# Spreading the projection work of a pair of token blocks over two attention units

## What is computed

```python
x: (32, 256, 128)                 # 32 batches, 256 tokens, width 128; 16 heads of 8
def _mha(q, k, v, ...):
    qp = (q @ wq.T + bq) * dh ** (-0.5);  kp = k @ wk.T + bk;  vp = v @ wv.T + bv
    s = einsum('bqhd,bkhd->bhqk', qh, kh)
    return einsum('bhqk,bkhd->bqhd', softmax(s), vh).reshape(B, Lq, D) @ w_out.T + b_out
# local: attention over axis 0 windows of 40 on the layer-normed x (with B = 32 only rows
# 0 to 31 of axis 1 and all 32 of axis 0); global: attention inside each of the 32 batches
x = layernorm(x + local + global)
x = layernorm(x + moe(x))         # top-1 routing over 8 experts, 1024 tokens each, 128-512-128
```

## Time and profile before

| | |
|---|---|
| median of 3 runs | 719.67 us (717.74 to 720.22) |
| the profiled execution's own time | 713.15 us |
| its span, first to last instruction | 711.4 us |
| TensorE busy (matmuls) | 633.0 us, 89% |
| VectorE busy | 561.1 us, 79% |
| ScalarE busy | 485.8 us, 68% |
| GpSimd busy | 445.1 us, 63% |
| mean granted TensorE clock | 0.949 |

### The profile page before, as it was taken

One profiled execution on the slowest core, in us unless ns is written; L12 is line 12 of the kernel. 1 busy time (PEld: TensorE's weight loads), 2 busy tenths in 40 slices (PEclk: granted clock), 3 DMA queues, 4 the chain that ended last, 5 costly groups with the idle time before them and its releaser, 6 DMA issues.

```text
span 711.4 us, 18732 instructions
## 1 busy us (share of the span) xinstructions
PE 633.0 (89%) x6430; PEld 353.5 (50%) x6430; DVE 561.1 (79%) x1722; ACT 485.8 (68%) x1095; POOL 445.1 (63%) x813
## 2 busy tenths in 40 slices
PE   3478999999999999999999999999999369999993
PEld 2344554445454454444544444444444237677682
DVE  7566899999999999999899998998972206776776
ACT  2226678888888988888878888888888234354431
POOL 5414434578788787787877877675667702544546
PEclk9657999999999999999999999999999569999997
DMA  5696889975648747666466565673401022333321
GB/s 114 157 214 173 215 232 194 249 178 124 168 134 184 176 99 208 165 140 164 111 158 179 120 160 144 131 176 73 86 26 35 27 65 73 108 97 105 96 86 40
DMA packets 143960, 95.70 MB, mean 135 GB/s; under 512 B 11885, under 2 KB 139718, under 8 KB 143865
## 3 DMA queue, kind: packets, MB, share of 16 engines
q1 hardware_dynamic: 138728, 85.82, 50.2%
q0 software_dynamic: 4096, 7.81, 3.8%
q10 hardware_dynamic: 1040, 0.87, 0.5%
HBM read 47.70 MB, written 45.74 MB: 131 GB/s over the span
## 4 chain that ended last, share of the span: by engine, by line
PE 58%; DVE 27%; issue 6%; DMA 4%; SPq 2%; POOL 2%; ACT 2%; DVEq 0%; POOLq 0%; ACTq 0%
DVE mx L1040 15%; PE ps_o L613 11%; PE ps_b L586 9%; PE ps_a L1487 7%; PE ps_b L1481 4%; PE ps_a L568 4%; PE ps_m L644 3%; PE ps_f L522 3%; PE ps_m L659 2%; PE ps_f L517 2%; PE ps_f L527 2%; PE ps_a L1481 2%; PE ps_f L1481 2%; PE ps_m L638 2%; DVE rest L1012 2%
## 5 line engine op out<-in xcount | busy, mean ns | idle before, releaser
L1040 DVE TENSOR_REDUCE mx<-ps_a 128x2 f32<-128x512 f32 (+1 forms) x576 | 360.3, 654 | 44.9 <-PE ps_a L568 43.1
L839 ACT ACTIVATE prob<-ps_b 128x512 f32<-128x512 f32 (+1 forms) x576 | 301.2, 580 | 66.4 <-PE ps_b L586 65.3
L568 PE MATMUL ps_a<-ks,qs 56*128 56x256 bf16 (+1 forms) x1152 | 186.0, 272 | 12.0 <-DMA ks<-stack 6.2
L586 PE MATMUL ps_b<-qs,ks 59*128 59x256 bf16 (+1 forms) x1152 | 187.7, 269 | 6.5 <-DMA qs<-mT 1.7
L613 PE MATMUL ps_o<-prob,vp 128*32 128x256 f32 (+1 forms) x2304 | 170.2, 379 | 0.4 <-ACT prob L839 0.4
L586 PEld LDWEIGHTS ps_b<-qs,ks 59*128 59x128 bf16 x1152 | 80.5, 95 | 105.2 <-ACT prob L839 64.5
L1631 POOL DMA_INDIRECT out<-res,dest x64 | 62.3, 973 | 76.5 <-DVE res L1604 61.1
L1334 POOL DMA_INDIRECT routed<-row,slot x64 | 67.2, 1050 | 47.7 <-issue 27.4
L568 PEld LDWEIGHTS ps_a<-ks,qs 56*128 56x128 bf16 x1152 | 75.2, 95 | 25.2 <-DVE mx L1040 13.1
L613 PEld LDWEIGHTS ps_o<-prob,vp 128*32 128x32 f32 x2304 | 49.1, 108 | 57.1 <-issue 48.6
L1487 PE MATMUL ps_a<-w_sb,prob 128*128 128x128 f32 x512 | 59.7, 275 | 2.1 <-ACT prob L1539 2.1
(11 more groups left out here) (153 smaller groups left out, 999.2 us busy)
## 6 DMA issues: line engine op xcount, KB each, us to landing
stack<-part SPq DMA_DIRECT2D x36, 384.0 KB, 3.3
qs<-stack SPq DMA_DIRECT2D x72, 192.0 KB
ks<-stack SPq DMA_DIRECT2D x72, 192.0 KB
stack<-part SPq DMA_DIRECT2D x36, 256.0 KB, 3.6
stack<-part SPq DMA_DIRECT2D x36, 128.0 KB, 4.3
routed<-empty SPq DMA_DIRECT2D x8, 520.0 KB, 4.6
rows_sb<-routed SPq DMA_DIRECT2D x16, 260.0 KB, 3.9
xt<-x SPq DMA_DIRECT2D x16, 256.0 KB, 3.1
```

Source lines behind the costliest of these rows:

```text
L568: ins = nc.tensor.matmul(ps_a[:, n % 3, qt * S:qt * S + keys.stop - keys.start], qs[half, b, hp, qt * P:(qt + 1) * P], ks[half, b, hp, key ...
L586: ins = nc.tensor.matmul(ps_b[:, 1 - e, kt * n:(kt + 1) * n], ks[half, u % STACKS, hp, kt * P:(kt + 1) * P], qs[half, u % STACKS, hp, quer ...
L839: nc.scalar.activation(prob[:, hp, half * n:(half + 1) * n], ps_b[:, half, 0:n], ACT.Exp).then_inc(exp_done, 1)
L1040: nc.vector.reduce_max(mx[:, u % 2, :, col], ps_a[:, n % 3].rearrange("p (t k) -> p t k", t=2)[:, :, 0:k], axis=AX).then_inc(max_done, 1)
```

## The change

It moves instructions within the two units of a pair; the products and their sizes are the same, except that ScalarE's `second_part` of a pair (one instruction of 128 x 1024) becomes two of 128 x 512.

On TensorE `turn_x` goes from step 1 of the even unit to the end of step 7 of the odd unit before it (for the first such pair ahead of the loop). q goes from steps 3 and 4 to 2 and 3, k from step 7 alone to 6 and 7, v from step 2 alone to 2 and 3 of the odd unit. On ScalarE `scale_shift` goes from behind exponential 2 to behind exponential 0; `second_part_q` stands in the even unit behind exponential 6, `second_part_k` in the odd one behind exponential 2; the two halves of v are placed one exponential later each; `norm_again` of an odd unit goes one exponential later. On VectorE `take_rest_k` stands ahead of maximum (1, 1) in place of maximum (2, 0).

```diff
--- before.py
+++ after.py
@@ -683,13 +683,11 @@
                     pe.wait_ge(y_ready, min(u - 1, U))
                     pe.wait_ge(logits_read, batch(u - 3) + 1)
                     count_tokens(u - 3)
-                if first is not None:
-                    turn_x(first, 0)
-                    turn_x(first, 1)
             if hp == 2:
                 if second is not None:
                     project_in(second, "v", 0)
-                    project_in(second, "v", 1)
+                if first is not None:
+                    project_in(first, "q", 0)
                 if there(u - 1):
                     if routes(u - 3):
                         pe.wait_ge(counts_copied, batch(u - 3) + 1)
@@ -706,8 +704,10 @@
                     else:
                         pe.wait_ge(mT_ready, u + 1)
                     turn_max(u + 1)
+                if second is not None:
+                    project_in(second, "v", 1)
                 if first is not None:
-                    project_in(first, "q", 0)
+                    project_in(first, "q", 1)
             if hp == 4:
                 if there(u):
                     p_v(u, 0, 1)
@@ -719,8 +719,6 @@
                     turn_oN(u - 1)
                 if routes(u - 2):
                     turn_x1(u - 2)
-                if first is not None:
-                    project_in(first, "q", 1)
             if hp == 5:
                 if there(u):
                     p_v(u, 1, 0)
@@ -728,15 +726,20 @@
                     logits(u - 2)
                 if there(u - 1):
                     project(u - 1)
-            if hp == 6 and there(u):
-                p_v(u, 1, 1)
-                p_v(u, 2, 0)
+            if hp == 6:
+                if there(u):
+                    p_v(u, 1, 1)
+                    p_v(u, 2, 0)
+                if first is not None:
+                    project_in(first, "k", 0)
             if hp == 7:
                 if there(u):
                     p_v(u, 2, 1)
                 if first is not None:
-                    project_in(first, "k", 0)
                     project_in(first, "k", 1)
+                if first_pair(u + 1) is not None:
+                    turn_x(first_pair(u + 1), 0)
+                    turn_x(first_pair(u + 1), 1)
 
         pe.wait_ge(first_loaded, 16 * len(needed_first))
         turn_first(0)
@@ -772,6 +775,8 @@
                 turn_max(0)
         project_in(OPEN, "v", 0)
         project_in(OPEN, "v", 1)
+        turn_x(AHEAD, 0)
+        turn_x(AHEAD, 1)
         for u in range(U + 3):
             for hp in range(8):
                 score_half(u, hp, 0)
@@ -813,6 +818,14 @@
             nc.scalar.copy(part[:, first:first + 12].rearrange("p (h s t) n -> p s h t n", h=2, s=2)[:, :, halves, 1],
                            rest[:].rearrange("p s (h n) -> p s h n", h=2)[:, :, halves]).then_inc(part1_ready, 1)
 
+        def second_part_q(p):
+            act.wait_ge(rest_q, upto(p))
+            nc.scalar.copy(part_of(p, 1), by_unit(rest[:, 0]))
+
+        def second_part_k(p):
+            act.wait_ge(rest_k, upto(p))
+            nc.scalar.copy(part_of(p, 4), by_unit(rest[:, 1])).then_inc(part1_ready, 1)
+
         def place_v(p, h):
 
             act.wait_ge(projected_v, p + 1)
@@ -893,6 +906,8 @@
             first, second = first_pair(u), second_pair(u)
             if there(u):
                 exponential(u, 0)
+            if first is not None:
+                scale_shift(first)
             if second is not None:
                 first_part_k(second)
             if there(u):
@@ -903,16 +918,12 @@
                 copy_o(u - 1)
             if there(u):
                 exponential(u, 2)
-            if first is not None:
-                scale_shift(first)
             if second is not None:
-                second_part(second)
+                second_part_k(second)
             if there(u):
                 exponential(u, 3)
             if there(u + 1):
                 copy_max(u + 1)
-            if second is not None:
-                place_v(second, 0)
             if routes(u - 2) and batch(u - 2) >= 3:
                 number_rows(batch(u - 2))
             if u == LU:
@@ -926,13 +937,20 @@
             if first is not None:
                 first_part_q(first)
             if second is not None:
-                place_v(second, 1)
+                place_v(second, 0)
             if there(u):
                 exponential(u, 5)
-            if routes(u - 2):
+            if second is not None:
+                place_v(second, 1)
+            elif routes(u - 2):
                 norm_again(u - 2)
             if there(u):
                 exponential(u, 6)
+            if first is not None:
+                second_part_q(first)
+            if second is not None and routes(u - 2):
+                norm_again(u - 2)
+            if there(u):
                 exponential(u, 7)
             if routes(u - 2):
                 gate_exp(u - 2)
@@ -1134,11 +1152,12 @@
                 expert_mask(u - 3)
             if at == (1, 0) and routes(u - 3):
                 gate_sum(u - 3)
-            if at == (1, 1) and routes(u - 3):
-                gate(u - 3)
-            if at == (2, 0):
+            if at == (1, 1):
                 if second is not None:
                     take_rest_k(second)
+                if routes(u - 3):
+                    gate(u - 3)
+            if at == (2, 0):
                 if late is not None:
                     input_stats(late, (2, 3) if late > AHEAD + 1 else (0, 1, 2, 3))
             if at == (3, 0):
```

## The result

The changed kernel takes 716.31 us in the median (713.73 to 719.65, 19 runs) against 719.39 us (716.38 to 724.15, 18 runs) of the kernel before on the same chip: ratio 0.9957, 95% interval 0.9938 to 0.9975. A nineteenth run of the kernel before took 962.15 us, a slow one, and is left out. That is 3.1 us less, where 6.8 were forecast: the sign and the range were right, the size was less than half.

A forecast was written before the change was run, and what follows sets the result against it. Bound: the hand-over between TensorE and the two readers of its scores. Waits fall 0.50 us a pair: 6.0 over twelve pairs, 0.40 last odd unit, 0.4 first three, sum 6.8, so 712.9 us; 8 in 10 from 706.5 to 720.5.

The forecast's parts named there:

- TensorE's waits: Waits of TensorE in a pair's two units: 1.36 us before, 0.86 after, so 0.50 less a pair.
- step 0: Even unit, second maxima product: its 0.25 us wait goes, since `turn_x` moves ahead and VectorE catches up.
- Step 1's second half: Even unit, second half of the scores, waiting for exponential 0: 0.22 of its 0.33 us wait stays.
- Step 2's: Even unit, second half of the scores: new 0.36 us wait, as `scale_shift` delays exponential 1.
- Step 3: Even unit, second half of the scores: its 0.22 us wait goes, with q put in the step before.
- It adds no product on TensorE, so its load stays.: TensorE over a pair: with no product added, its load was taken as unchanged, and only waits were priced.
- ScalarE's split copies: `second_part` as two copies of 512 columns: 0.04 to 0.26 us more for ScalarE a pair, nothing on the path.
- VectorE doesn't hold the period: Answers the rival that VectorE's queue keeps the period at 28.78 us, giving 719.3 us; chance 0.13.
- More than that: Rival: the three new waits don't appear and all 1.36 us a pair go, time 701.8 us; chance 0.10.
- Slower: Rival: `scale_shift` delays the output copies, so `turn_o` waits; a pair loses 0.3 us, time 723.3 us; chance 0.14.
- The first three pairs: Pairs beside the local units, where the chain goes through `qs<-mT`: 0.4 us gained for all three, between nothing and 1.2.
- the last unit: Last odd unit, after the twelve whole pairs: its wait of 0.40 us goes.

The follow-up runs named there:

- set 4: Changed kernel, rest sooner, k in one group, and the kernel before, run together on a chip without late releases: changed 0.9952, kernel before 0.9981.
- v and k whole: Changed kernel but all of v in step 2 and all of k in step 7: 703.33 us, ratio 0.9843; again in set 3, 0.9918.
- rest sooner: Kernel before with only `take_rest_k` one maximum sooner: 707.34 us, ratio 0.9914; again in set 4, 0.9899.
- set 2's last kernel: Changed kernel with v and k in one group each, `scale_shift` behind exponential 1, q whole in step 3: 716.2 us, ratio 0.997.
- set 3: Kernel before, v and k whole, changed kernel, and v alone in one group, on a chip with late releases: changed 0.9955, kernel before 1.0023.
- set 2: Changed kernel and three variants of its q, k, v grouping or `scale_shift`, on a chip with late releases: changed 713.28 us, ratio 0.993.

## Why the prediction was right in sign and off in size

**TensorE's waits: right, and better than forecast.** TensorE's timeline of the changed kernel in set 4, the even unit's steps 0 to 3, second halves of the scores and what stands around them:

```profile
303.06 0.28 PE L586 MATMUL ps_b<-qs,ks 59*128 59x256 bf16 x1
...
303.60 0.64 PE L613 MATMUL ps_o<-prob,vp 128*32 128x256 f32 x8
304.20 0.28 PE L586 MATMUL ps_b<-qs,ks 59*128 59x256 bf16 x1
...
304.69 0.28 PE L586 MATMUL ps_b<-qs,ks 59*128 59x256 bf16 x1
...
305.84 0.28 PE L586 MATMUL ps_b<-qs,ks 59*128 59x256 bf16 x1
...
306.33 0.28 PE L586 MATMUL ps_b<-qs,ks 59*128 59x256 bf16 x1
...
307.72 0.28 PE L586 MATMUL ps_b<-qs,ks 59*128 59x256 bf16 x1
...
308.26 0.64 PE L613 MATMUL ps_o<-prob,vp 128*32 128x256 f32 x8
308.91 0.29 PE L623 MATMUL ps_m<-ident_bf,mpart 128*48 128x128 bf16 x2
```

Read as in the prediction: step 0 takes 0.54 from 303.06, no wait (forecast: gone). Step 1's second half stands at 304.69 and not 304.47: 0.22 (forecast 0.22). Step 2's at 306.33 and not 306.11: 0.22 (forecast 0.36). Step 3 has none (forecast: gone). `turn_max` comes 0.07 behind the `p_v` of 0.58 (forecast 0.10). In the odd unit it comes at 295.05, 0.68 behind a `p_v` that starts at 294.37: 0.10 (forecast 0.18). Sum 0.61 where I had 0.86; these waits fell by 0.75 and not by 0.50. Put the other way, from `scale_shift` I feared 0.36 and got 0.22, the ordinary wait of a step without much fill. And `take_rest_k` gave 0.44 for 0.40.

**The step that failed: "It adds no product on TensorE, so its load stays."** The count stayed, the time didn't. A group of projection products costs something for itself, and the sum had this term at nothing: measured it is 0.20 us a pair for k's second group and 0.24 for v's. To see it, take each of TensorE's groups in the two kernels of set 4 from its start to the start of the next:

| group, us in a pair | before | changed |
|---|---|---|
| v (L517) | 0.96 | 0.55 + 0.64 |
| k (L527) | 1.06 | 0.63 + 0.63 |
| q (L522) | 0.64 + 0.53 | 0.54 + 0.63 |
| `turn_x` (L499) | 0.57 | 0.59 |
| `turn_o` (L631), two units | 0.53 + 0.60 | 0.53 + 0.53 |
| the row's turning (L651), two units | 0.31 + 0.22 | 0.31 + 0.31 |
| scores, over all steps | 10.66 | 9.75 |
| `p_v`, over all steps | 9.22 | 9.09 |

The scores and `p_v`, which hold the waits, fell by 1.04 us. The groups rose: v 0.23, k 0.20, the row's turning 0.09 (a half of q stood behind it before), `turn_o` -0.07, `turn_x` 0.02, together 0.47, and the counts' small products (0.30 before, 0.47 now, with what waits in them) 0.17. 0.64 less 1.04 is -0.40; measured 28.78 to 28.36. The warning stood in the rows of before, had I looked for it: q was in two groups already, 0.64 and 0.53 for two products each, and k in one, 1.06 for four. The same rows show when no price is paid: where a group stands directly behind another group of projections or turnings. In the chain of the kernel before (set 4), which counts from the end of what stands ahead, q's first half follows `turn_max` and its second half the row's turning:

```profile
308.61 0.63 PE ps_f L522 x2
...
310.94 0.43 PE ps_f L522 x2
```

The whole 0.20 is gone there. (In the table, which counts from start to start, half of it shows in the group and half in the one ahead: 0.53 for q, 0.22 and not 0.31 for the row's turning.) By this reading what counts is the number of stretches of such work between the scores, `p_v` and the small bf16 products. A pair has 9 in the kernel before, 11 in the changed one, 9 again with v and k whole; two more at 0.20 are 0.40, an estimate, where 0.44 was measured.

Two experiments price it independently of the table: v whole against halves is 0.24 (27.92 to 28.16), k 0.20 (28.16 to 28.36).

**What made it work nonetheless.** From rest sooner (28.34) to v and k whole (27.92) the moves of x, q and ScalarE's copies are worth 0.42; the halves of v and k take 0.44 back. The change is thus the sooner `take_rest_k` and two sets of moves that cancel. My forecast had 0.10 for everything beside `take_rest_k` (0.64 of waits won, 0.54 of new ones); measured it is 0.42 less 0.44. That the forecast of a pair came near, 0.50 for 0.42, is luck: two mis-sized terms have opposite signs.

**ScalarE's split copies: right in size.** In set 4 the two halves take 0.69 (at 293.73) and 0.65 us (at 315.26) where one took 1.12, 0.22 more, inside the bounds of 0.04 to 0.26. ScalarE is busy for 24.45 of 28.36 us, so there is room for it; that it costs nothing on the path is argued, no run has the split alone.

The Trainium skill, "Perfetto Trace Analysis", section "Optimizing Scalar/DVE Operations", says of ScalarE and VectorE that breaking up instructions may help where they aren't saturated but make others idle. No run here shows whether splitting ScalarE's copy did so; the 1.4 us in 15 pairs that the prediction has from its figure is 0.09 a pair, and the rows show 0.22. TensorE, busy for 28.09 of 28.36 us, isn't what the section speaks of; there two groups for one cost 0.2 us.

**The rivals.** VectorE doesn't hold the period: it went to 28.36, and on to 27.92 with VectorE's order as in the changed kernel and its busy time at 26.45. "More than that" didn't come, since each step with little fill keeps its 0.22 to 0.27. "Slower" was near: its mechanism is what set 2's last kernel has.

**The first three pairs: 0.4 us forecast, no gain instead.** In set 4 the changed kernel's stretch from the loop's fourth `take_rest_k` to the end is 560.82 us long, against 566.02 of before, 5.2 less; adding the 0.6 by which this mark now stands sooner in its unit, 5.8, where I had 6.4. The whole is only 2.9 less (spans 710.7 and 713.6). So 2.9 us went before that. But 2.0 of them stand already in the first `take_rest_q`, ahead of the loop and of everything that the change moves: it starts at 42.93 before and at 44.96 after, and over all 18 profiles it scatters from 39.99 to 44.96. From there to the loop's fourth `take_rest_k` it is 102.67, 106.21 and 104.65 us before, 104.28, 103.36, 104.37 and 104.92 after the change, and 100.77 and 101.95 where only `take_rest_k` is sooner. With the 0.6 the change loses 0.9 us there in set 4 and 0.3 on the mean, inside the scatter; the simple edit wins 2.5.

One thing that works against the change can be read in set 3's changed kernel: ScalarE's copy of the maxima, SyncE's transfer of it, and TensorE behind it, at the start of unit 2.

```profile
72.26 0.37 ACT L858 COPY mT<-ps_m 48x256 bf16<-48x256 bf16 x1 [0.27 <-PE ps_m L623]
...
74.87 1.62 SPq L406 DMA_DIRECT2D qs<-mT  x2
...
79.58 0.28 PE L586 MATMUL ps_b<-qs,ks 59*128 59x128 bf16 x1 [2.08 <-DMA qs<-mT]
```

The same in the kernel before, set 4, where TensorE's wait stands a unit later:

```profile
71.95 0.37 ACT L845 COPY mT<-ps_m 48x256 bf16<-48x256 bf16 x1 [0.27 <-PE ps_m L623]
...
72.34 1.62 SPq L406 DMA_DIRECT2D qs<-mT  x2
...
89.62 0.23 PE L586 MATMUL ps_b<-qs,ks 59*128 59x128 bf16 x1 [1.33 <-DMA qs<-mT]
```

Before, the transfer is issued as soon as its copy is done, 0.02 behind it. After, it is issued 2.24 behind it, since SyncE's queue has other transfers ahead of it. Counted over units 2 and 3, TensorE waits for `qs<-mT` 0.81, 1.58 and 1.33 us in the three profiles of the kernel before, 1.82, 1.97, 2.08 and 1.44 in those of the changed one, and 1.41 and 0.93 with rest sooner. So the change adds about 0.6 us of this wait, but it isn't new, and set 4's changed kernel has it in unit 3 and not in unit 2. Such a wait can be paid for a second time. In set 3's changed kernel TensorE is busy for 0.42 of the 2 us from 78 to 80, and from 80 to 86 the granted clock is 0.50, that is 1.2 GHz, where two of q's products take 1.22 us (at 82.59) and not 0.70. This doesn't tell the kernels apart, though: from 72 to 97 us the mean granted clock is 0.93, 0.89 and 0.90 before and 0.86, 0.93, 0.86 and 0.97 after the change, and 1.00 in both profiles of rest sooner. I had said that the chain goes through `qs<-mT` there and then priced only what I took away, not what the moved `turn_max` and SyncE's queue behind it do. That the queue keeps the gain away is read, not tested: no kernel here changes the loop and leaves the first units alone.

**The rest of the gap.** Twelve pairs at 0.42 are 5.0 us, the last unit 0.4. With 0.3 to 0.9 lost in the first pairs that is 4.5 to 5.1, where the ratios of the four comparisons give 3.1, 5.0, 3.2 and 3.4 us. Of the 3.7 us between forecast and result the pairs are thus 1.0 (twelve at 0.08) and the first three pairs 0.7 to 1.3. Part of the scatter between the comparisons is the clock: the changed kernel's runs had a mean granted clock 0.0026 above those of the kernel before in set 2, 0.0034 below in set 3 and 0.0012 below in set 4. With the slopes within each set (0.46, 0.23 and 0.37 us for 0.001) the three differences come to 3.8, 4.0 and 3.9 us, by estimate. About one us stays unexplained between the periods and the timed runs.

## What to carry to other kernels

Splitting a group of products to fill a short step has a price per group even if no product is added; compare the rows of one group of four with two of two before moving anything, and move whole groups first. Price each edit alone: here one moved VectorE instruction gave all that the change gave, and with x, q and ScalarE's work moved but v and k left whole the kernel is 1.6% faster than before (0.9843; 0.9918 on a chip with late releases), better than both kernels. And before two profiles are compared, run both kernels on one chip: the same kernel's period differed by 0.20 to 0.53 us from chip to chip, as much as the effect in question. A stretch that the change doesn't touch, here the units without pair work, tells whether two profiles stand on the same footing; measure it from a mark to the same mark of the next unit.

## What the hardware showed that was not expected

- A group of projection products costs about 0.2 us for itself between scores and exponentials' products: 4 products of 128x256 1.06 us in one group, 1.26 in two; 8 of 128x128 0.96 and 1.19. Directly behind another group of projections or turnings it doesn't: two products of q take 0.43 us there in the chain, and 0.63 elsewhere. Why the first group costs it is open.
- Late releases: on some chips the scores of step 7 are seen by ScalarE 1.2 to 1.3 us after their recorded start and not 0.48, in every odd unit of a pair and in the units without pair work, whichever of the kernels runs. VectorE and SyncE's queue go on at the same moment: 300.29 and 300.33 us beside ScalarE's 300.31 in the changed kernel's first profile, for scores of 299.05. Even units have 0.56 to 0.77 in the same step in six of the nine profiles. There are 21 to 32 in a profile there, 0 to 2 elsewhere. Of the four sets' chips two had them, and so did the profile of the result. The cause is open.
